# Graph attention with layer norm on one core: mixing x before gcn_w instead of after it

## What is computed

```python
hi = x @ W1[:384] + emb[adj] @ W1[384:] + b1      # per pair of nodes
hj = x @ W2[:384] + emb[adj] @ W2[384:] + b2
A = softmax(where(adj != 0, sum(hi * hj, -1), -1e9))
h = relu((A @ x) @ gcn_w + gcn_b)
out = layernorm(x + h @ Wo + Wo_b)                # over 384, eps 1e-5
```

## Time and profile before

| | us |
|---|---|
| median of 3 executions | 379.76 (379.12 to 379.9) |
| the profiled execution's own time | 380.05 |
| its span in the trace | 378.0 |
| TensorE busy | 372.1 |
| VectorE, GpSimd, ScalarE busy | 220.7, 153.3, 142.1 |

### The profile page before, as it was taken

One profiled execution on the slowest core, in us unless ns is written; L12 is line 12 of the kernel. 1 busy time (PEld: TensorE's weight loads), 2 busy tenths in 40 slices (PEclk: granted clock), 3 DMA queues, 4 the chain that ended last, 5 costly groups with the idle time before them and its releaser, 6 DMA issues.

```text
span 378.0 us, 10088 instructions
## 1 busy us (share of the span) xinstructions
PE 372.1 (98%) x4011; PEld 340.0 (90%) x4011; DVE 220.7 (58%) x584; ACT 142.1 (38%) x342; POOL 153.3 (41%) x133
## 2 busy tenths in 40 slices
PE   9999999999999999999999999999999999999994
PEld 4789898999989899998989989898998989999994
DVE  2546264674646567464666646476664646756596
ACT  1725442514334252333415234351423425142433
POOL 1333454270815418072450807236080632608035
PEclk9999999999999999999999999999999999999998
DMA  7922023508052260805317071441706245170105
GB/s 228 332 96 85 21 81 81 185 10 255 5 180 84 45 219 5 232 27 164 99 32 231 0 210 53 131 133 19 245 0 192 72 103 161 20 247 2 43 2 211
DMA packets 34851, 42.88 MB, mean 113 GB/s; under 512 B 10128, under 2 KB 29072, under 8 KB 34832
## 3 DMA queue, kind: packets, MB, share of 16 engines
q1 hardware_dynamic: 33600, 41.13, 36.3%
q10 hardware_dynamic: 1232, 1.49, 1.2%
HBM read 30.03 MB, written 12.58 MB: 113 GB/s over the span
## 4 chain that ended last, share of the span: by engine, by line
PE 98%; DVE 0%; POOL 0%; issue 0%
PE banks L447 18%; PE banks L449 18%; PE banks L448 18%; PE banks L547 9%; PE banks L548 9%; PE banks L553 9%; PE banks L526 7%; PE banks L471 7%; PE banks L571 2%; PE banks L560 1%; PE banks L506 1%; PE banks L581 0%; PE banks L597 0%; PE banks L592 0%; DVE xt_sb L1052 0%; PE banks L540 0%
## 5 line engine op out<-in xcount | busy, mean ns | idle before, releaser
L1160 POOL TENSOR_TENSOR x_sb<-x_sb,wob_sb 128x1536 f32<-128x1536 f32 x15 | 52.8, 3519 | 174.8 <-DVE weights L989 163.0
L958 DVE SCALAR_TENSOR_TENSOR hs_lo<-banks,hs_hi 128x256 fp32r<-128x256 f32 x90 | 32.6, 418 | 67.3 <-ACT hs_hi L818 67.2
L447 PE MATMUL banks<-gcn_hi,xt_hi 128*128 128x386 f32 x192 | 66.7, 347 | 0.0
L448 PE MATMUL banks<-gcn_lo,xt_hi 128*128 128x386 f32 x192 | 64.8, 338 | 0.0
L449 PE MATMUL banks<-gcn_hi,xt_lo 128*128 128x386 f32 x192 | 64.8, 337 | 0.0
L547 PE MATMUL banks<-wo_hi,hs_hi 128*128 128x384 f32 x180 | 60.9, 338 | 0.0
L553 PE MATMUL banks<-wo_hi,hs_lo 128*128 128x384 f32 x180 | 60.5, 336 | 0.0
L548 PE MATMUL banks<-wo_lo,hs_hi 128*128 128x384 f32 x180 | 60.5, 336 | 0.0
L759 ACT ACTIVATE gt_sb<-banks,r_sb 128x512 f32<-128x512 f32 x48 | 33.1, 689 | 70.2 <-PE banks L449 70.1
L447 PE MATMUL banks<-xt_hi,m_hi 128*128 128x512 f32 x144 | 57.4, 398 | 0.0
L449 PE MATMUL banks<-xt_hi,m_lo 128*128 128x512 f32 x144 | 56.8, 394 | 0.0
(11 more groups left out here) (101 smaller groups left out, 513.9 us busy)
## 6 DMA issues: line engine op xcount, KB each, us to landing
xt_sb<-in_x_t_dram SPq DMA_DIRECT2D x15, 768.0 KB, 4.6
x_sb<-in_x_dram SPq DMA_DIRECT2D x15, 768.0 KB, 5.6
out_dram<-y_sb SPq DMA_DIRECT2D x30, 384.0 KB, 5.8
adj_sb<-in_adj_dram SPq DMA_DIRECT2D x32, 64.0 KB, 2.3
xt_sb<-in_x_t_dram SPq DMA_DIRECT2D x2, 384.0 KB, 8.4
xt_sb<-in_x_dram SPq DMA_DIRECT2D x1, 768.0 KB, 4.9
w1t_sb<-in_w_t_dram ACTq DMA_DIRECT2D x3, 192.0 KB, 5.6
w2t_sb<-in_w_t_dram SPq DMA_DIRECT2D x3, 192.0 KB, 3.4
```

The lines of the kernel that those rows point to most:

```text
L447: pe.matmul(acc, a_hi, b_hi, start=first, stop=False)
L448: pe.matmul(acc, a_hi, b_lo, start=False, stop=False)
L1160: pool.tensor_tensor(x_home(g, slot), x_home(g, slot), wob_sb[:].rearrange("p (o n) -> p o n", o=1).to_broadcast([P, PAIRS, HID]), ALU.add ...
```

## The change

The mixing takes x itself (x_sb, rows as loaded) and gcn_w comes behind it. `value`, `value_out`, hg_sb and the row of gcn_b go. ScalarE's `split_z` and VectorE's `low_z` split the mixed x (z), `gemm(g-1)` multiplies it by gcn_w as 27 matmuls of 512 columns right behind the scores of group g, with gcn_w stationary. gcn_b is now added by ScalarE with the relu (`hidden`), which also writes less_sb, the high half minus gcn_b; VectorE's `low_hidden` makes max(gemm, -gcn_b) minus less_sb. The row term comes from VectorE: `row_products` multiplies rows of x with u_row (u spread over all partitions by one matmul with ones at the start) and sums them. The outputs of group g-1 come last in the body, behind the projection of g+1; they are normalised one body later than before. x is loaded twice, into x_sb for the mixing and into y_sb for the sum with the output; GpSimd adds Wo_b there, behind the normalising of the group that had the buffer. wo_lo is made by GpSimd in body 1 instead of by VectorE at the start. The banks are given out anew, and out_x goes. Removed lines are left out below where the listing above shows them.

```diff
-        PROJ_BANK = [bank[4], bank[2], bank[3]]
-        MIX_BANK = ((6, 6, 4), (7, 7, 5))
-        VALUE_BANK = bank[1:5]
         score = bank[0]
-        PROJ0_BANK = bank[5:8]
-        PROJ1_BANK = [bank[5], bank[2], bank[3]]
-        GB_BANK = bank[2]
+        PROJ_BANK = bank[4:7]
+        PROJ1_BANK = bank[1:4]
+        U_BANK = bank[7]
+        MIX_BANK = ((4, 4, 6), (5, 5, 7))
...
-                return bank[q - 1]
+                return bank[(3, 2)[q - HALVES]]
             if static(g, LAST - 1):
-                return bank[(3, 1, 2, 3)[q]]
+                return bank[(3, 1, 6, 7)[q]]
             if static(g, LAST):
-                return bank[(1, 2, 3, 0)[q]]
-            return bank[(5, 6, 7, 1)[q]]
+                return bank[(3, 1, 2, 4)[q]]
+            return bank[(1, 2, 3, 1)[q]]
+        def gemm_bank(g):
+            return [bank[2], bank[4], bank[5]] if static(g, LAST) else GEMM_BANK
...
+            sp.dma_start(x_sb[:, 0], x_rows[0]).then_inc(x_loaded[0], 16)
+            load_adj(0, 0)
+            sp.dma_start(gcn_sb[:], gcn_w.rearrange("(c p) n -> p c n", p=P)).then_inc(gcn_loaded, 16)
+            sp.dma_start(x_sb[:, 1], x_rows[1]).then_inc(x_loaded[1], 16)
+            sp.dma_start(wo_sb[:], wo_w.rearrange("(c p) n -> p c n", p=P)).then_inc(wo_loaded, 16)
+            load_adj(1, 1)
             sp.dma_start(wob_sb[:], wo_b.to_broadcast([P, HID])).then_inc(wob_loaded, 16)
+            for slot in range(2):
+                sp.dma_start(y_sb[:, slot], x_rows[slot]).then_inc(y_loaded[slot], 16)
...
+                if not static(g, 0) and before(g, LAST):
+                    sp.wait_ge(mix_mm, g)
+                    sp.dma_start(x_sb[:, 1 - par], x_rows[g + 1]).then_inc(x_loaded[1 - par], 16)
...
+                for h in range(HALVES):
+                    sp.wait_ge(y_ready, HALVES * (g - 2) + h + 1)
+                    sp.dma_start(out_rows[g - 2][:, 2 * h:2 * h + 2], y_sb[:, par, 2 * h:2 * h + 2]).then_inc(stored[par], 16)
+                sp.wait_ge(stored[par], 1 + 16 * HALVES * half(g, par))
+                sp.dma_start(y_sb[:, par], x_rows[g]).then_inc(y_loaded[par], 16)
...
+            def gemm(g):
+                for f in range(C):
+                    fs = slice(f * P, (f + 1) * P)
+                    if static(g, LAST):
+                        pe.wait_ge(added, PAIRS * (g - 1))
+                    elif not (static(g, 0) or static(g, LAST - 1) and f == C - 1):
+                        pe.wait_ge(added, PAIRS * (g - 1) + f + 2)
+                    for n, c in enumerate(BLOCKS):
+                        if f == 0:
+                            pe.wait_ge(zlo, C * g + n + 1)
+                        mm = three(gemm_bank(g)[f][:, 0:GT], gcn_hi[:, c, fs], gcn_lo[:, c, fs],
+                                   z_hi[:, c, :], z_lo[:, c, :], n == 0, n == C - 1)
+                    mm.then_inc(gemm_mm, 1)
...
+                if static(g, 0):
+                    pe.wait_ge(gt_ready, C)
+                elif not static(g, LAST):
+                    pe.wait_ge(gt_ready, C * (g + 2))
...
+            def out(g, q):
+                if q < HALVES or static(g, LAST):
+                    pe.wait_ge(hslo, C * (g + 1))
+                if static(g, LAST) and q < HALVES:
+                    pe.wait_ge(added, PAIRS * (g - 1) + q + 1)
+                elif q == PAIRS - 1 and static(g, LAST - 2):
+                    pe.wait_ge(hslo, C * (g + 1) + 1)
+                elif q == PAIRS - 1 and before(g, LAST - 2):
+                    pe.wait_ge(added, PAIRS * g + 1)
                 ts = slice(q * P, (q + 1) * P)
+                high, low = hs_home(g)
+                for n, c in enumerate(BLOCKS):
+                    mm = three(out_bank(g, q)[:, 0:HID], high[:, c, ts], low[:, c, ts], wo_hi[:, c, :], wo_lo[:, c, :],
+                               n == 0, n == C - 1)
+                mm.then_inc(out_mm, 1)
...
             pe.wait_ge(c12_sb_ready, 1)
+            pe.wait_ge(ones_ready, 1)
             pe.matmul(score[:, K_AT:K_AT + C], ones[:].to_broadcast([P, P]), c12_sb[:],
                       start=True, stop=True).then_inc(rk_mm, 1)
             pe.wait_ge(m_lo_ready, C)
+            pe.wait_ge(u_sb_ready, 1)
+            pe.wait_ge(xt0_lo, C)
             pe.wait_ge(xlo, 1)
+            proj(0, 0, PROJ_BANK, range(C))
+            pe.wait_ge(u_diag_ready, 1)
+            pe.matmul(U_BANK[:, 0:HID], ones[:].to_broadcast([P, P]), u_diag, start=True, stop=True).then_inc(u_mm, 1)
+            proj(0, 0, PROJ_BANK, range(C, C * C))
+            pe.wait_ge(xlo, 2)
+            proj(1, 1, PROJ1_BANK, range(2))
             def body(g, par):
                 if not static(g, 0):
                     mix(g - 1, 1 - par)
                 score_stage(g, par)
+                if static(g, 0):
+                    proj(1, 1, PROJ1_BANK, range(2, C * C - 1))
+                    pe.wait_ge(ident_ready, 1)
+                    turn(g)
+                    proj(1, 1, PROJ1_BANK, range(C * C - 1, C * C))
+                    return
+                if static(g, 1):
+                    pe.wait_ge(gcn_lo_ready, 1)
+                gemm(g - 1)
+                turn(g)
                 if static(g, LAST):
+                    out(g - 2, 3)
                     mix(g, par)
+                    out(g - 1, 0)
+                    out(g - 1, 1)
+                    gemm(g)
+                    out(g - 1, 2)
+                    out(g - 1, 3)
+                    for q in range(PAIRS):
+                        out(g, q)
                     return
+                pe.wait_ge(xlo, g + 2)
+                proj(g + 1, 1 - par)
+                if static(g, 1):
+                    pe.wait_ge(wo_lo_ready, 1)
+                for q in range(PAIRS - 1 if static(g, LAST - 1) else PAIRS):
+                    out(g - 1, q)
...
+            def split_z(g):
                 act.wait_ge(mix_mm, g + 1)
                 for n, f in enumerate(BLOCKS):
                     if n == C - 1:
-                        act.wait_ge(hslo, C * g + 1)
-                    act.activation(by_graph(hs_home(g)[0][:, f, :]), mixed(f), ACT.Relu).then_inc(hshi, 1)
+                        act.wait_ge(zlo, C * g + 1)
+                    act.copy(by_graph(z_hi[:, f, :]), mixed(f)).then_inc(zhi, 1)
+            def hidden(g):
+                if static(g, 0):
+                    act.wait_ge(ngb_ready, 1)
+                else:
+                    act.wait_ge(hslo, C * g)
+                for f in range(C):
+                    act.wait_ge(gemm_mm, C * g + f + 1)
+                    act.activation(hs_home(g)[0][:, f, :], gemm_bank(g)[f][:, 0:GT], ACT.Relu,
+                                   bias=gb_sb[:, f:f + 1]).then_inc(hshi, 1)
+                    act.wait_ge(hshi, C * g + f + 1)
+                    act.activation(less_sb[:, f, :], f32(hs_home(g)[0][:, f, :]), ACT.Identity,
+                                   bias=ngb_sb[:, f:f + 1]).then_inc(less_ready, 1)
             def body(g, par):
                 if not static(g, 0):
+                    split_z(g - 1)
+                weigh(g)
+                if static(g, 0):
+                    project_out(1, PROJ1_BANK, range(C - 1))
+                else:
                     hidden(g - 1)
-                weigh(g)
+                act.wait_ge(turn_mm, g + 1)
+                act.copy(at_sb[:], score[:, 0:MIX]).then_inc(at_ready, 1)
+                if static(g, 0):
+                    project_out(1, PROJ1_BANK, range(C - 1, C))
                 if before(g, LAST - 1):
                     split_x(g + 2, par)
                 if before(g, LAST):
-                    row_terms(g + 1, 1 - par)
-                act.wait_ge(turn_mm, g + 1)
-                act.copy(at_sb[:], score[:, 0:MIX]).then_inc(at_ready, 1)
-                if before(g, LAST):
-                    project_out(g + 1, PROJ1_BANK if static(g, 0) else PROJ_BANK)
+                    if not static(g, 0):
+                        project_out(g + 1)
+                    row_terms(g + 1)
                 else:
+                    split_z(g)
+                    normalise_last(LAST - 2, 1, 1, (0, 1))
+                    normalise_last(LAST - 2, 1, 1, (2, 3))
                     hidden(g)
...
+            def row_products(g, slot):
+                dve.wait_ge(x_loaded[slot], 16 * (half(g, slot) + 1))
+                if not static(g, 0):
+                    dve.wait_ge(srow_ready, g)
+                for q in range(PAIRS):
+                    a = dve.scalar_tensor_tensor(products[:, q, :], x_sb[:, slot, q, :], 1.0, u_row[:], ALU.mult, ALU.mult,
+                                                 accum_out=xu_row[:, q:q + 1])
+                a.then_inc(xu_ready, 1)
...
+            def low_z(g):
+                for n, f in enumerate(BLOCKS):
+                    dve.wait_ge(zhi, C * g + n + 1)
                     for h in range(HALVES):
```

(84 more changed lines are left out.)

364 lines of the change are left out of this document (88 added, 276 removed).

## The result

| | us |
|---|---|
| changed kernel, median of 4 | 385.7 (384.38 to 385.97) |
| kernel before, beside it, median of 4 | 379.83 |
| ratio, 95% interval | 1.0154 [1.0131, 1.0177] |
| span of the profiled execution | 383.7 (before: 378.0) |

A forecast was written before the change was run, and what follows sets the result against it. TensorE, busy 372.1 of 378.0 us, was taken as the bound, so only its work and waits count. Terms -1.8 + 2.7 + 0.8 + 1.8 + 1.3 - 0.65 + 0.6 = +4.75 us gave 384.5 us, range 380.2 to 388.5.

The forecast's parts named there:

- gcn_w on 512 columns: In each group, 27 matmuls instead of 36 save 0.11 us, -1.8 us over 16 groups.
- Rival D: Steps bound by weight loads: 27 steps would take 4.73 us a group, 355 us in all; chance 0.02.
- The wait ahead of gcn_w: Behind the mixing, TensorE waits for halves of mixed x: 0.18 us a body, +2.7 in 15 bodies (0 to +5.2).
- rival A: Halves arrive in time, so TensorE never stands still behind a mixing: faster, 378.7 us; chance 0.15.
- Opening: From the start to the mixing of group 0, which starts at about 30.7 us: +0.8 us.
- Order on ScalarE in body 1: Behind the first mixing, ScalarE's x_t cast and row terms precede mixed x's high half: +1.8 us once (0.5 to 3).
- GpSimd and VectorE in body 1: With wo_lo on GpSimd, VectorE's four row products still go back to back, outputs not delayed: taken as 0.
- rival C: In body 1 row products alternate with GpSimd's passes, outputs start 3.3 us late: 387.8, up to 391 us; chance 0.18.
- The last body: ScalarE does the whole hidden stage before at_sb, and an output waits 0.2 for a low half: +1.3 us (0.5 to 2).
- out_x: At the end, the out_x matmuls go: -0.65 us.
- Addition before the last statistics: At the end, the last quarter again needs an addition before its statistics: +0.6 us.

The follow-up runs named there:

- e2: e1 with ScalarE's row terms of group 1 moved behind the high halves of group 0's mixed x; 380.26 us, ratio 1.0006.
- e10: The changed kernel with only ScalarE's row terms of group 0 put ahead of the wo_hi cast in the opening; 384.65 us, ratio 1.0128.
- e1: The changed kernel with one wait more: in body 1 GpSimd starts wo_lo only behind VectorE's four row products; 381.44 us, ratio 1.0036.
- e6: e1 without the wait that holds GpSimd's passes behind normalising in bodies 1 to 14; 465.71 us, ratio 1.2245.
- e7: The changed kernel with ScalarE's at_sb copy of the last body ahead of the last third of hidden(14); 385.39 us, ratio 1.0134.
- e11: e10 with three TensorE matmuls of zeros into an unused bank, ahead of group 0's outputs in body 1; 383.43 us, ratio 1.0096.

## Why the prediction was right, and where it was not

- **gcn_w on 512 columns**, forecast -0.11 a group: shown. Steps of 0.229, and 6.41 to 6.33 with 0.04 of wait left in it. Rival D (steps bound by weight loads) is out: its steps would be 0.175, and while weight loads went from 340.0 to 319.7 busy us the matmuls' time did not follow.
- **The wait ahead of gcn_w**, 0.18 a body: mis-sized, measured 0.04, some 2 us too much over the kernel. The data came as reckoned: z_lo ends 4.49 us behind the mixing's start (171.67 + 2.17 - 169.35), before 4.51. The failing step is "Each block is then late by up to its load". The loads did wait, 2.2 us in all behind z_lo; the second row is the load of the third block in the group shown above:

```profile
L457 PEld LDWEIGHTS banks<-z_hi,gcn_hi 128*128 128x128 f32 x144 | 27.0, 188 | 11.4 <-DVE z_lo L934 2.2 <-issue 1.7
173.88 0.19 PEld L457 LDWEIGHTS banks<-z_hi,gcn_hi 128*128 128x128 f32 x1 [0.17 <-DVE z_lo L934]
```

  This load started 0.11 ahead of its matmul (173.99), where the others start 0.23 ahead, and yet the matmul came 0.24 behind the one before it (173.75) instead of 0.229. So a load's delay was passed on by 0.01 and not by its 0.19. For the regular groups rival A was right: they became faster, 22.20 where 22.3 to 22.4 was named.
- **Opening** +0.8: 30.41 for the 30.7 forecast, +0.5, within a spread of 29.95 to 31.45 between traces.
- **Order on ScalarE in body 1** +1.8: shown, 1.7 in the trace, of which e2 removed 1.2 (the row terms); the 0.46 left is the cast of x_t for group 2, which still stands ahead of z_hi and can itself be late, as in e10.
- **GpSimd and VectorE in body 1**, taken at 0 with 3.3 kept as rival C: it happened, 2.4 us. The failing step is the choice: "VectorE has its four lined up while GpSimd must first see the signal". GpSimd started at 40.38, 0.16 behind VectorE's first product, and queued passes don't keep the port; they alternate. The mechanism and the bound were in the text, the wrong one of two cases was taken.
- **The clock**: no term for it, so it stood at nothing. +1.6 behind the 2.25 us wait, in most executions. This and the line above, 4.0 together, are what e1 takes away.
- **The last body** +1.3: 0.7. hidden's passes were 0.67 and 0.72 us; at_sb came 12.0 us behind the mixing instead of 12.6, and TensorE wanted it at 11.6 instead of 11.4. **out_x** -0.65: 6.24 for 6.88. **Addition before the last statistics** +0.6: 0.55.

The sum was near the result by luck, because errors cancel: about 2 us too much in the regular groups, about 4 too little in body 1, and 0.9 over in the opening and last body. The sign was right partly for a wrong reason: the forecast had the regular groups as a loss of 0.9 us, and they were a gain of 1.0. e2 shows that without body 1's two collisions (ScalarE's order, GpSimd beside VectorE) the change is no loss that can be told from noise.

## What to carry to other kernels

When work moves in an engine's list, the regular groups are the easy part; reckon each written-out body at either end by itself, since a guard that holds in the loop may be missing there (here one missing wait on GpSimd cost 4.1 of 5.7 us). Let passes of GpSimd and VectorE that both read SBUF be ordered by a semaphore, with the urgent ones first: without that order this kernel is 22% slower. A price for a stall of TensorE should include what its clock may do behind it: here 2.4 us of waiting cost 1.6 more.

## What the runs showed that was not expected

- Half clock behind a standstill: after a wait of 2.25 us ten of twelve output steps were 0.32 instead of 0.17 apart (granted 0.51, the 1.2 GHz level), in all 1.6 us; in e6, after 4.46 us, eleven steps and more. An equal wait (2.27 us in e7) left the clock at full level, and so did waits of 1.63 and 1.88. With matmuls of zeros in the wait ahead of the outputs none of 11 executions had a low mean clock, but e11 shows that the zeros can't be the whole reason. Why equal waits differ stays open.
- When the fall comes ahead of a wait for another engine, as in e10's trace, it is free: the same 1.6 us were inside a wait.
- VectorE and GpSimd alternate operation by operation: 3.03 and 3.88 us for passes of 0.55. GpSimd pays too: 2.93 and 3.84 for 2.70 and 3.52 when alone (e1).
- The load of Wo at the start lands at times that differ by over 1 us between executions; whoever stands behind its cast inherits that.
